# DLRM interaction tower: an eleventh table read by one-hot products, three one-hot slots, and gathers that start before the last one of the group ahead has landed

## What is computed

```python
e = jnp.stack([tbl_f[ids[:, f]] for f in range(26)], axis=1)          # 2048 x 26 x 128
combined = jnp.concatenate([e, r_dense_x[:, None, :]], axis=1)        # 27 features
interact = jnp.einsum('bfd,bgd->bfg', combined, combined)             # a 27 x 27 Gram matrix per sample
z = interact[:, triu_i, triu_j]                                       # its 351 pairs
h = jnp.maximum(jnp.concatenate([z, r_dense_x], 1) @ W_top1 + b_top1, 0)   # 479 -> 512
h = jnp.maximum(h @ W_top2 + b_top2, 0)                                # 512 -> 256
y = h @ W_top3                                                        # 256 -> 1
```

## Time and profile before

| | us |
|---|---|
| median of 3 runs | 556.9 (556.6 to 562.27) |
| the profiled execution, its own time | 551.39 |
| its span, first to last instruction | 549.5 |
| PE / weight loads / DVE / ACT / POOL busy | 476.3 / 436.3 / 315.8 / 233.9 / 248.9 |
| mean granted TensorE clock | 0.957 |

### The profile page before, as it was taken

How to read it: one execution, slowest core, us unless ns; L and a number is a source line. 1 busy time by engine, 2 the same in 40 slices (tenths; PEclk the granted TensorE clock), 3 DMA queues, 4 the chain that set the end, 5 groups by cost and what they waited for, 6 DMA issues and landing times.

```text
span 549.5 us, 9188 instructions
## 1 busy us (share of the span) xinstructions
PE 476.3 (87%) x3544; PEld 436.3 (79%) x3544; DVE 315.8 (57%) x503; ACT 233.9 (43%) x755; POOL 248.9 (45%) x266
## 2 busy tenths in 40 slices
PE   3786677998888998899898998989998898899988
PEld 3676576897887888789788888879897887889977
DVE  6994137564467535675366654775367543676252
ACT  3532225443444343534435344443545335354454
POOL 6435554455555554455545445554554545420000
PEclk9998569899899998999999999999999899999999
DMA  8551111111111111111111111111111101100000
GB/s 291 189 151 40 37 38 34 39 39 48 35 39 35 44 39 35 39 38 44 35 35 38 35 49 40 39 35 43 35 40 35 39 24 40 35 21 0 1 2 1
DMA packets 12511, 25.80 MB, mean 47 GB/s; under 512 B 4931, under 2 KB 6603, under 8 KB 12458
## 3 DMA queue, kind: packets, MB, share of 16 engines
q0 software_dynamic: 8192, 16.79, 11.5%
q1 hardware_dynamic: 4276, 8.42, 4.8%
HBM read 25.18 MB, written 0.01 MB: 46 GB/s over the span
## 4 chain that ended last, share of the span: by engine, by line
PE 71%; DVE 10%; DMA 6%; POOL 5%; issue 5%; ACT 2%; another core or an unknown queue 1%; POOLq 0%; DVEq 0%; ACTq 0%
PE x_ps L437 23%; PE gram_ps L453 23%; PE tail_ps L508 13%; DVE onehot L617 8%; DMA raw<-in_tbl,ids_sb 6%; POOL raw L398 4%; PE x_ps L415 4%; PE ids_ps L423 3%; PE tail_ps L478 2%; DVE gram L279 2%; PE tail_ps L487 2%; PE tail_ps L514 2%; DVE split_weights L638 1%; ACT xt L552 0%
## 5 line engine op out<-in xcount | busy, mean ns | idle before, releaser
L398 POOL DMA_INDIRECT raw<-in_tbl,ids_sb x256 | 245.6, 959 | 234.7 <-DMA raw<-in_tbl,ids_sb 161.4
L617 DVE TENSOR_TENSOR onehot<-ids_ps,row_no 128x1024 fp32r<-128x1024 f32 (+1 forms) x160 | 206.7, 1303 | 77.3 <-PE x_ps L437 50.1
L437 PE MATMUL x_ps<-onehot,hot_hi 128*128 128x256 f32 x688 | 185.0, 302 | 24.3 <-DVE onehot L617 17.7
L437 PE MATMUL x_ps<-onehot,hot_lo 128*128 128x256 f32 x688 | 174.4, 286 | 0.0
L437 PEld LDWEIGHTS x_ps<-onehot,hot_hi 128*128 128x128 f32 x688 | 133.3, 194 | 33.2 <-issue 16.4
L453 PE MATMUL gram_ps<-xt 128*128 128x108 f32 x1024 | 137.6, 289 | 14.1 <-DVE gram L279 11.2
L453 PEld LDWEIGHTS gram_ps<-xt 128*128 128x128 f32 x1024 | 129.7, 203 | 21.6 <-ACT gram L279 13.9
L279 DVE COPY gram<-gram_ps 32x104 f32<-32x104 f32 x256 | 68.6, 268 | 117.1 <-PE gram_ps L453 99.7
L437 PEld LDWEIGHTS x_ps<-onehot,hot_lo 128*128 128x128 f32 x688 | 133.6, 194 | 0.0
L279 ACT COPY gram<-gram_ps 32x104 f32<-32x104 f32 x256 | 60.4, 236 | 103.0 <-PE gram_ps L453 73.3
L552 ACT COPY xt<-x_ps 128x256 f32<-128x256 f32 x80 | 49.7, 621 | 99.7 <-PE x_ps L437 91.4
(11 more groups left out here) (48 smaller groups left out, 267.9 us busy)
## 6 DMA issues: line engine op xcount, KB each, us to landing
raw<-in_tbl,ids_sb POOLq DMA_INDIRECT x256, 2.5
table_home<-in_tbl SPq DMA_DIRECT2D x4, 512.0 KB, 8.8
table_home<-in_tbl SPq DMA_DIRECT2D x2, 640.0 KB, 4.2
raw<-in_tbl SPq DMA_DIRECT2D x2, 512.0 KB, 4.7
dense_sb<-in_dense_t SPq DMA_DIRECT2D x8, 128.0 KB
gram<-in_tbl SPq DMA_DIRECT2D x1, 640.0 KB, 12.2
h<-in_tbl SPq DMA_DIRECT2D x1, 512.0 KB, 11.2
h<-in_w SPq DMA_DIRECT2D x1, 256.0 KB
```

Of the source, the lines that this page charges most:

```text
L398: nc.gpsimd.indirect_dma_start(out=raw[k][:, f, :], out_offset=None, in_=tables[f], in_offset=bass.IndirectOffsetOnAxis(ap=ids_sb[:, t, f: ...
L437: last = nc.tensor.matmul(ps, table[:, chunk_at[j] + c, :], onehot[:, p % RING, c - a, :], start=(c == 0 and table is hot_hi), stop=(c == ...
L617: nc.vector.tensor_tensor(onehot[:, p % RING, 0:n, :], ids_ps[:, it % 2, :].unsqueeze(1).to_broadcast([P, n, BLOCK]), row_no[chunks[it % n ...
```

## The change

- `HOT` 10 to 11: one 1250-row table (10 chunks) moves from the gathers to the one-hot products. Cold groups are then 4, 4, 4 and 3 gathers.
- `RING` 2 to 3 one-hot slots; `DENSE` 3 to 2 buffers for the dense input.
- A group of gathers waits for all but the last gather of the group ahead (the wait on `last_in` goes).
- Ids rows: not one 10 x 2048 array rounded once, but 256 columns for each block in 128 partitions (the rest zero), loaded and rounded block by block in two buffers; `pick` becomes the rounded identity, of which one column is read with stride zero as weights.
- The tail is placed by `(n + TAIL_OVER) / total` and may run over into the Gram fills of tile 0.
- `zt` goes: DVE makes `zt_lo` straight from PSUM and then frees the bank, where ACT's second copy did.
- For want of room, new homes for tables; the second half of w2 is loaded into `h1` only after the first weight split (`rest_weights_in`).

```diff
-HOT = 10
+HOT = 11
-DENSE = 3
-RING = 2
+DENSE = 2
+RING = 3
-SPREAD = 1.2
+TAIL_OVER = 3
...
-        scale = SPREAD * n / tail_at[-1] if tail_of else 0
+        scale = (n + TAIL_OVER) / tail_at[-1] if tail_of else 0
+        left = [(at * scale, step) for step, at in zip(tail_of, tail_at)]
...
         for i in range(n):
-            steps += [step for step, at in zip(tail_of, tail_at) if i - 1 < at * scale <= i]
+            while left and left[0][0] <= i:
+                steps.append(left.pop(0)[1])
...
         for i in range(n_gram):
+            while left and left[0][0] <= n + i:
+                steps.append(left.pop(0)[1])
             steps += turns[1][i * n_turn // n_gram:(i + 1) * n_turn // n_gram]
             steps.append(("gram", m + i))
...
                 copy(zt_hi[0:kz[j], j, :].rearrange("p (g s) -> p g s", s=QUAD), src).then_inc(zt_rounded, 1)
-                last = copy(zt[0:kz[j], j, :].rearrange("p (g s) -> p g s", s=QUAD), src)
+                return
...
+            if kind == "zt":
+                dve.wait_ge(zt_rounded, h * n_kz + j + 1)
...
+                nc.vector.tensor_tensor(lo, src, hi.bitcast(F32), ALU.subtract).then_inc(zt_split, 1)
+                dve.wait_ge(zt_split, h * n_kz + j + 1)
+                dve.sem_inc(tail_copied[bank], 1)
...
             sp.dma_start(ids_sb[:, :, :], ids).then_inc(ids_in, 16)
-            sp.dma_start(ids_row_in, hot_ids).then_inc(ids_row_landed, 16)
+            sp.wait_ge(ids_raw_cleared, 1)
+            for h in range(2):
+                ids_load(h)
...
+                if k == 1:
+                    for h in range(1, DENSE):
+                        dense_load(h)
+                    sp.wait_ge(weights_split, 1)
...
             for h in range(blocks):
+                if h + 2 < blocks:
+                    sp.wait_ge(ids_row_ready, h + 1)
+                    ids_load(h + 2)
...
+            nc.gpsimd.memset(ids_raw[:, :, :], 0).then_inc(ids_raw_cleared, 1)
             nc.gpsimd.memset(ident[:, :], 0.0).then_inc(consts_ready, 1)
-            nc.gpsimd.memset(pick_in, 0.0).then_inc(consts_ready, 1)
...
                     if g > 0:
                         pool.wait_ge(rows_in[k][g - 1], (t // RAW + 1) * (16 * (len(turn_groups[g - 1]) - 1)))
-                        pool.wait_ge(last_in[k][g - 1], (t // RAW + 1) * 16)
                     elif t > 0:
                         pool.wait_ge(rows_in[(t - 1) % RAW][n_turn - 1],
                                      ((t - 1) // RAW + 1) * (16 * (len(turn_groups[n_turn - 1]) - 1)))
-                        pool.wait_ge(last_in[(t - 1) % RAW][n_turn - 1], ((t - 1) // RAW + 1) * 16)
...
-                    last = nc.tensor.matmul(ids_ps[:, it % 2, :], pick[:, j, :],
-                                            ids_row[:, h * BLOCK:(h + 1) * BLOCK], start=True, stop=True)
+                    last = nc.tensor.matmul(ids_ps[:, it % 2, :], pick[:, j:j + 1].to_broadcast([P, P]),
+                                            ids_row[:, h % 2, :], start=True, stop=True)
...
+            def ids_round(h):
+                dve.wait_ge(ids_raw_in[h % 2], (h // 2 + 1) * 16)
+                copy(ids_row[:, h % 2, :], ids_raw[:, h % 2, :]).then_inc(ids_row_ready, 1)
...
+                if kind == "ids" and rounded <= min(2 * what[0] + 3, items - 1) // nh:
+                    ids_round(rounded)
+                    rounded += 1
```

More of the change, by code:

```diff
@@ L121, in plan @@
         for i in range(n):
-            steps += [step for step, at in zip(tail_of, tail_at) if i - 1 < at * scale <= i]
+            while left and left[0][0] <= i:
+                steps.append(left.pop(0)[1])
             steps += hot_steps(first + i, first + i + 1)
             steps += [turn for turn, at in zip(turns[0], turn_at) if at == i]
-        steps += [step for step, at in zip(tail_of, tail_at) if at * scale > n - 1]
-        assert len([s for s in steps if s[0] == "tail"]) == len(tail_of)
         m = h * gram_block
         for i in range(n_gram):
+            while left and left[0][0] <= n + i:
+                steps.append(left.pop(0)[1])
             steps += turns[1][i * n_turn // n_gram:(i + 1) * n_turn // n_gram]
             steps.append(("gram", m + i))
+        assert len([s for s in steps if s[0] == "tail"]) == len(tail_of)
         m += n_gram
@@ L176, in build @@
         hot_lo = sb("hot_lo", [P, chunk_at[nh], P], F32R)
[L177 to L178 removed]
+        ids_raw = sb("ids_raw", [P, 2, BLOCK], I32)
+        ids_row = sb("ids_row", [P, 2, BLOCK], F32R)
+        pick = sb("pick", [P, P], F32R)
         row_no = {n: sb(f"row_no{n}", [P, n]) for n in row_kinds}
@@ L182, in build @@
         z = sb("z", [P, QUAD, half_pairs[0]])
-        zt = sb("zt", [P, n_kz, BLOCK])
+        h1 = sb("h1", [P, m1, BLOCK])
+        h2 = sb("h2", [P, m2, BLOCK])
+        with nc.sbuf_tensor("table_home", [P, 2 * (n_kz * d1 + m1 * d2 + n_kz * BLOCK + m1 * BLOCK)], F32) as table_home:
+            pass
+        split_weights = sb("split_weights", [P, 2 * (n_kz * d1 + m1 * d2)], F32R)
         zt_hi = sb("zt_hi", [P, n_kz, BLOCK], F32R)
         zt_lo = sb("zt_lo", [P, n_kz, BLOCK], F32R)
-        h1 = sb("h1", [P, m1, BLOCK])
         h1_hi = sb("h1_hi", [P, m1, BLOCK], F32R)
         h1_lo = sb("h1_lo", [P, m1, BLOCK], F32R)
[L189 to L192, removed]
         w1z_hi, w1z_lo, w2_hi, w2_lo = (
@@ L204, in build @@
                 h1[:, :, :].rearrange("p m n -> p (m n)"), gram[:, :, :].rearrange("p q g -> p (q g)")]
-        table, part = 8 * P, 10 * P
-        homes = [(0, 0), (0, table), (1, 0), (1, part), (1, 2 * part), (1, 3 * part), (2, 0), (3, 0), (1, 0), (1, part)][:nh]
+        homes = [(0, 0)] + [(1, 10 * P * n) for n in range(5)] + [(2, 0), (3, 0)] + [(1, 10 * P * n) for n in (5, 0, 1)]
+        homes = homes[:nh]
         hot_in = [flat[b][:, at:at + n * P] for (b, at), n in zip(homes, chunks)]
@@ L229, in build @@
         hot_landed = [sem(f"hot_landed{j}") for j in range(nh)]
-        ids_row_landed = sem("ids_row_landed")
+        ids_raw_in = [sem(f"ids_raw_in{k}") for k in range(2)]
+        ids_raw_cleared = sem("ids_raw_cleared")
         dense_in = [sem(f"dense_in{k}") for k in range(DENSE)]
         weights_in = sem("weights_in")
+        rest_weights_in = sem("rest_weights_in")
         weights_rounded = sem("weights_rounded")
@@ L325, in tail_split @@
             kind, j = key
-            if kind in ("zt", "h1"):
-                bank = tail_bank[key]
+            bank = tail_bank[key]
+            if kind == "zt":
+                dve.wait_ge(zt_rounded, h * n_kz + j + 1)
+                src = tail_ps[bank][0:kz[j], 0:BLOCK].rearrange("p (s g) -> p g s", s=QUAD)
+                hi, lo = (part[0:kz[j], j, :].rearrange("p (g s) -> p g s", s=QUAD) for part in (zt_hi, zt_lo))
+                nc.vector.tensor_tensor(lo, src, hi.bitcast(F32), ALU.subtract).then_inc(zt_split, 1)
+                dve.wait_ge(zt_split, h * n_kz + j + 1)
+                dve.sem_inc(tail_copied[bank], 1)
+            elif kind == "h1":
                 dve.wait_ge(tail_copied[bank], h * tail_per[bank] + tail_nth[key] + 1)
[L329 to L332, removed]
+                nc.vector.tensor_tensor(h1_lo[:, j, :], h1[:, j, :], h1_hi[:, j, :].bitcast(F32),
+                                        ALU.subtract).then_inc(h1_split, 1)
         @block.sync
@@ L354, in _ @@
             sp.dma_start(b2_sb[:, :], b2).then_inc(weights_in, 16)
-            for k in range(2):
+            for k, landed in ((0, weights_in), (1, rest_weights_in)):
+                if k == 1:
+                    for h in range(1, DENSE):
+                        dense_load(h)
+                    sp.wait_ge(weights_split, 1)
                 sp.dma_start(w2_in[k].rearrange("p (k n) -> p k n", k=2),
-                             w2.rearrange("(k p) n -> p k n", p=P)[:, 2 * k:2 * k + 2, :]).then_inc(weights_in, 16)
-            for h in range(1, DENSE):
-                dense_load(h)
+                             w2.rearrange("(k p) n -> p k n", p=P)[:, 2 * k:2 * k + 2, :]).then_inc(landed, 16)
             for h in range(blocks):
+                if h + 2 < blocks:
+                    sp.wait_ge(ids_row_ready, h + 1)
+                    ids_load(h + 2)
                 if h + DENSE < blocks:
@@ L579, in _ @@
                         act.wait_ge(hot_split, nh)
-                        for hi, _, src in weight_parts:
+                        for n, (hi, _, src) in enumerate(weight_parts):
+                            if n == len(weight_parts) - 1:
+                                act.wait_ge(rest_weights_in, 16)
                             copy(hi, src).then_inc(weights_rounded, 1)
```

28 lines of the change are left out of this document (14 added, 14 removed).

## The result

The changed kernel takes 628.9 us (median of 4, 624.65 to 633.75) where the kernel before takes 558.5 (556.6 to 562.27): a ratio of 1.136, 95% interval 1.128 to 1.144. I had forecast 540, 524 to 559, and faster with a chance of 0.73. The profiled execution has a span of 631.6 us, 82 more than before, and a granted clock of 0.887.

What follows compares the result with a forecast made beforehand. Prediction: after a 73 us start set by gathers, PE bounds seven blocks of about 64 us, with holes. Terms -11.2 - 2.4 + 2 + 16.8 - 18.2 - 3.6 = -16.6 took 556.9 to 540 us, range 524 to 559.

Steps and rivals of the forecast that it cites:

- POOL is faster than its consumer: Mid-run blocks: eight gather groups take 58 us against a 64.0 us block, so POOL is held by PE's transposes.
- Start: the gathers: First Gram stage: groups start 1.25 us sooner over seven handoffs, plus one issue less per tile; -11.2 us.
- the third: Rival, z steps: DVE in fixed order ends last and delays PE's reuse of tail banks; +31, 571 us; chance 0.10.
- gathers at the start: First Gram stage: last transposes start near 60.9 instead of 72.14, as gathers are issued sooner; -11.2 us.
- clock in the first Gram stage: First Gram stage: PE kept busy holds its clock at the 2.4 GHz level; -2.4 us (0 to -4).
- late w2 part: Start: ACT and DVE wait for the w2 part loaded after the first weight split; +2 us (bounds 0 and 4).
- eleventh table: Every block: PE gets 10 more chunks of products, less two transposes; 2.4 us a block, +16.8 us over seven.
- third slot: One-hot handoff, every block: DVE uses its idle time on the next piece; 2.6 us a block, -18.2 us.
- tail placing: End of every block: a Gram fill covers PE's wait for ACT's last copy; 0.52 us a block, -3.6 us.
- the eight new ids casts: DVE's ids casts: each may hold a gather; with the first long cast gone, the sum 1 us lower, left out.
- Theory A: Expectation for the experiments: PE's signals are late while several gathers are under way, and the relaxed wait shortens the pause.

Runs made afterwards that it cites:

- e11: The changed kernel unaltered, timed again beside the kernel before at 555.2 us: 614.3 us, ratio 1.099.
- e8: The changed kernel with the full wait for the group ahead put back, beside the kernel before at 555.2 us: 558.4 us, ratio 1.003.
- e9: The kernel before with the relaxed wait alone, beside the kernel before at 555.2 us: 581.0 us (four runs, no interval).
- e2: The kernel before with the relaxed wait alone, beside the kernel before at 515.9 us: 501.5 us, ratio 0.973.
- e4: The kernel before with half the room for gather descriptors (2048 for 4096 bytes a partition): 513.0 us (one run), beside 515.9.
- e12: The changed kernel with one semaphore for each gather and at most two gathers under way: 521.2 us, ratio 0.934, beside 558.5.
- e14: As e12, the changed kernel with at most two gathers under way, but HOT back at 10: 497.4 us, ratio 0.892.
- e5: The changed kernel unaltered, beside the kernel before at 561.3 us: 614.4 us (four runs, no interval).
- e6: The changed kernel with HOT back at 10, beside the kernel before at 561.3 us: 571.8 us, ratio 1.021.
- e7: The changed kernel with RING back at 2, beside the kernel before at 561.3 us: 611.0 us, ratio 1.087.
- e15: As e12, the changed kernel with at most two gathers under way, but RING back at 2: 518.3 us, ratio 0.924.
- e10: The kernel before with one semaphore for each gather and never more than two under way, beside 555.2 us: 517.6 us, ratio 0.929.
- e13: The kernel before with one semaphore for each gather and never more than three under way, beside 558.5 us: 647.5 us, ratio 1.163.
- the first series: Full wait in the changed kernel; relaxed wait, two-gather limit or half descriptor room in the kernel before: 515.6, 501.5, 510.0, 513.0 us, beside 515.9.
- e1: The changed kernel with the full wait for the group ahead put back, beside the kernel before at 515.9 us: 515.6 us, ratio 0.999.
- the last series: Variants of e14 with two slots, the old tail placing or nine tables: ratios 0.940, 0.930, 0.937, beside the kernel before at 535.5 us.

## Why the prediction was wrong

**The step that failed** is what I drew from "POOL is faster than its consumer": that gathers issued sooner cost the others nothing, so that "Start: the gathers" is the only place where the relaxed wait counts. POOL was the faster one indeed (it waited 214.4 us for PE); the step from there to a cost of nothing was wrong. I priced an earlier gather by what it lands on and put at nothing what it does to the others. In its place the runs show PE's signals held up: in the condition of the result the relaxed wait costs 56 us in the changed kernel (e11 against e8), and alone in the kernel before 13 to 26 (e9). Of the rivals only the third looked for a loss, and it looked in DVE. It gave 571; DVE's waits for `zt_hi` are 3.8 us in all in the changed kernel, so it was not the cause either.

Term by term:

| term | predicted | measured |
|---|---|---|
| gathers at the start | -11.2, of it -8.75 for the relaxed wait | -10.2 for the relaxed wait with signals in time (62.02 in e2, 72.27 in e4); +16.7 in the changed kernel (88.85 against 72.14) |
| clock in the first Gram stage | -2.4, at its upper level | 0.93 in e2's stretch of 50 to 75 us; 0.68, then 0.50 in the changed kernel |
| late w2 part | +2 | ACT waited 1.8 us for it, 2.2 in e12 |
| eleventh table | +16.8 | +24 (e12 less e14), +32 to +43 with many late signals (e5 less e6) |
| third slot | -18.2 | none with eleven tables (e7, e15) |
| tail placing | -3.6 | not isolated within a series |
| late signals | not in the sum | +56 to the changed kernel (e11 less e8) |

The start is right in kind where the signals are in time, and a little small: e2 has ten tables and so no group of three, the sum has -8.75 - 2.4 = -11.2 for it, and it is 14.4 us faster than the kernel before. The third slot failed by a misreading that has the same root. At 224.25 DVE had idled 1.62 us for PE, and I took both slots for full. But the first of the two pieces from about 222 on the earlier trace rows was used up at 223.01; the trace has the update of its signal at 224.23, and DVE started 0.02 us later. In e4 the same piece starts 0.04 us after its slot was used up, and DVE had idled 0.43:

```profile
209.29 2.36 DVE L617 TENSOR_TENSOR onehot<-ids_ps,row_no 128x1024 fp32r<-128x1024 f32 x2 [0.43 <-PE x_ps L437]
```

A third slot can't give back the time in which a release is late. Why it gives nothing where the signals are mostly in time (e15) is not shown. The table's term was sized from PE alone; its two DVE pieces and its ids round trip may be what makes it 24, which no run separates.

The first gather took 1.13 us and not 1.92, with the long cast gone, and the mean of all stayed at 0.96: the cost of the eight new ids casts that I left out is not seen. By the rule of the Trainium skill that I had weighed (SBUF — State Buffer, "SBUF: two separate sides") the first was to be expected, and the trace agrees. The same page, section "Who interferes with whom", says "DMA never contends with a compute engine". That is about the ports of SBUF, and the runs don't speak against it: from e10 to e13, which differ only in the limit (and stand in two series), the kernel takes 25% longer, but DVE's and ACT's busy times stay (316.3 and 315.3 us, 233.4 and 232.1) and PE's rises 5% (470.5 to 493.5) with its granted clock down from 0.961 to 0.896. Apart from PE's clock the engines are not slower; the signals of PE are late.

**What is shown and what is open.** Shown: in the condition where the kernel before takes about 557 us, the limit on gathers, and with it how closely POOL issues them, sets how late PE's signals are, from 22 us in sum (limit of two) over 55 (groups of four with a rest) to 256 (limit of three, no rest until PE holds POOL), and the time follows: 518, 555 to 559, 647. The gathers themselves are not slower: group to group 7.1 us in e4, 7.2 in the earlier trace rows. That the number under way matters, as Theory A and the word "limit" suggest, is not shown, and the packets speak rather for the spacing; neither a limit of one nor a fixed pause without a limit was run. Not shown either: by what path the gathers hold the signals up, why a limit of two still leaves some late, and what the condition is. The same kernel took 516, 535 and 555 to 561 us in different series; within one series it stayed put.

On the condition the traces have one clue. In the four of the first series every semaphore update by an engine is in the records (1406 of 1406 in e1, counting semaphores with eight updates or more). In all the others 12 to 20% are missing (207 of 1352 in the kernel before), also in the last series, where few signals are late, and of the updates by DMAs far more: 2318 are recorded there and 4558 in e4, for the same kernel but for the descriptor room. So wherever signals are late, records of signals are missing too. Whether the profiler's own recording takes part in the lateness, no run tests.

Why the whole loss (56 us) is larger than that of the relaxed wait alone (13 to 26) I have not separated either. The changed kernel was never run where signals are in time; from e1 (0.999 with the full wait) and e2 (0.973 for the wait alone) an estimate there is some 500 us, which is only that. Of the 20 us between e14 and e10 (the kernel before, limit of two) the slot and the tail are not seen to explain more than a part; the `zt` and ids edits were not taken alone.

## What to carry to other kernels

An engine that is off the critical path still loads what all share: before letting it run ahead, ask what its transfers do to the others, and try spacing them first. Here a limit of two, which spaces the gathers, took 0.93 of the time of groups of four, and a limit of three, which doesn't, took 1.16. When waiters start together and late after work that had ended, and the profile names no releaser, measure from the end of the work to the start of its own waiter against the phase of the transfers, and match the two in order: the first copy after a fill need not be that fill's. The late signals were there in the trace of the kernel before. And time such kernels in more than one series, since a change may gain in one condition (e2, 0.973) and lose in another (e9).

## What the runs showed of the hardware

- Signals of PE (the increments with a matmul) reached ACT and DVE up to 33.8 us late while POOL issued 37 gathers in a row, one every 1.25 us (e13); signals of DVE and ACT in the same run at most 0.15 us. In the four runs of the first series none of PE's signals with a Gram fill was over 0.04 us late, with the gathers in groups of four in two of them.
- In the kernel before 16 of the 34 late fills are copied 5.70 to 5.79 us after the first gather of a group, whenever they ended.
- A 128-row gather of 64 KB takes 3.3 to 3.45 us from its issue to the next group's first issue in either condition (e1, e4, e8, the kernel before), and 2.2 us (median) to its last packet; the lateness is not in the gathers.
- Of the engines' semaphore updates 12 to 20% are missing from every trace but the four of the first series, which miss none.
